# Moving two quantisation passes, eight PSUM conversions and one scaling between ScalarE and VectorE in a quantised matmul kernel with a recurrent branch

## The chip, the cores and the metric

The kernel runs on all 8 cores of one Trainium2 chip. Each core has its own TensorE (PE), VectorE (DVE), ScalarE (ACT), GpSimd (POOL) and SyncE (SP, which issues the transfers here). Every core gets 2 of the 16 sequences and runs the same program. The time is the device time in microseconds (us) of the slowest core.

## The reference, cut to what matters

```python
x = L0_attn_x                                   # (16, 2048, 2048) f32
xn = layernorm(x)
# branch 1: s
xn1 = layernorm(xn) * gamma + beta
u   = xn1 @ W_in + b_in                         # rank 8
h   = scan(u, sigmoid(decay_logit))             # h[t] = decay * h[t-1] + u[t]
x2  = xn + h @ W_out + b_out + xn1 * D_skip
xn2 = layernorm(x2) * gamma + beta
s   = x2 + relu(xn2 @ W_down + b_down) @ W_up + b_up     # rank 32
# branch 2: g
xq  = fake_quant(xn, 8 bits, per row)           # round(xn / scale) * scale
kq  = fake_quant(kernel, 8 bits, per column)    # 2048 x 2048
y   = relu(xq @ kq + fake_quant(bias))
g   = silu(fake_quant(y, 8 bits, per row))
out = x + s * g
```

## The kernel before, in words

A prologue of some 470 us loads and quantises the 2048x2048 weight matrix, which then stays in SBUF as `kq` (bf16), and folds the small weights together. After it a core handles its 4096 rows in 32 chunks of 128 rows, which lie on the 128 partitions. There is one stream of instructions for each engine, in the order in which the Python code emits them; each instruction waits on semaphores for the ones that it depends on. An engine never overtakes within its own stream, so an instruction that waits holds up all that was emitted for its engine behind it. The emission order, with the functions of the code, is:

```
emit_pro(0)
for c in range(NCH):
    emit_mid(c)
    emit_big_half(c, 0)
    emit_mid2(c)
    emit_big_evacs(c, 0)
    emit_big_half(c, 1)
    if c + 1 < NCH: emit_pro(c + 1)
    emit_big_evacs(c, 1)
    emit_echunk(c)
```

- `emit_pro(c)`: load of x; statistics on DVE (L450 to L465); square root on ACT (L466); the normalised row `xn` in f32 on ACT (L478), its bf16 copy `xnb` on ACT (L483); the row's largest magnitude on DVE (L484) and from it the two quantisation scales (L485 to L488; `inv0` is L487).
- `emit_mid(c)`: T1, 16 matmuls with the identity that transpose `xnb` (L518) into two PSUM banks in turn, four to a bank, each bank converted to bf16 in `xnT` by ACT (`t1e`, L522, four of them); `q8`, ACT's pass from `xn` to 8-bit integers (L525); `qbf`, ACT's pass from those to bf16 (L527); T2, 16 transposing matmuls of `qbf` (L539) through the same two banks, converted by ACT into `ixqT` (`t2e`, L543, four of them). A bank is written again only when its last conversion is done. Then a small transpose of the scale row, which ACT copies out (`auge`, L558), and behind that copy the small transpose `r1T` on PE (L560), copied by DVE (`r1a`, L561). Then PE multiplies `xnT` with the small weights (L578, 16 matmuls), DVE runs the scan (L590), and four rounds of two matmuls and two DVE operations (L609 to L617) make x2.
- `emit_big_half(c, h)`: 32 matmuls of 128x128 by 128x512 against one half of `kq` (L710) and two for the bias (L716). The first half waits for x2, the second one for the first one's evacuation.
- `emit_mid2(c)`: squares on ACT (L641), a square root, small matmuls, s = x2 + ... on DVE (L687).
- `emit_big_evacs(c, h)`: DVE scales the result of a half out of PSUM into `t1` with its row maximum (L727, L730).
- `emit_echunk(c)`: DVE makes the two scales (`g1` to `g6`, L774 to L779). Then, for each half of 1024 columns: `e2` rounds `t1` times a scale to int32 (`qi`, L783, DVE), `e3` is Relu to bf16 (L789, ACT), `e4` is Silu (L792, ACT), `sg` multiplies with s (L797, POOL), `o` adds x (L801, POOL), and a transfer stores it. There is one buffer `qi`, one `r` and one `g`: the second half's e2 waits for the first half's e3, its e4 for the first half's sg.

Because e4 of chunk c's second half is emitted for ACT ahead of all that `emit_mid(c+1)` emits for ACT, the conversions L522 of chunk c+1 stand behind it.

Of the kernel before, what the change touches and what calls it, by code (L numbers as in the profile page):

```python
# [11 lines left out]
OP = mybir.AluOpType  # L12
AF = mybir.ActivationFunctionType
# [67 lines left out]
def build_nc(n_seq, seq_len):  # L81
# [39 lines left out]
    with es:  # L121
# [32 lines left out]
        cq128 = sb("cq128", [128, 1], F32)  # L154
        cm128 = sb("cm128", [128, 1], F32)
# [16 lines left out]
        t1_t = sb("t1", [128, D], F32)  # L172
        qi_t = sb("qi", [128, 1024], I32)
# [176 lines left out]
        for fi in range(ND):  # L350
            h = {}
# [77 lines left out]
        def emit_pro(c):  # L429
# [58 lines left out]
            v4 = V([v1], lambda e: e.tensor_single_scalar(st[:, 12:13], st[:, 10:11], 1.0 / 127.0, OP.mult))  # L488
            rc["inv0"] = v3
            rc["sc0"] = v4  # L490
            return

        def emit_mid(c):
# [12 lines left out]
            for g in range(4):  # L506
                bank = tb2[g % 2]
                for b in range(4):
                    j = 4 * g + b
                    deps = [rc["xnbd"], L["eyeb"]]  # L510
                    if b == 0:
                        if g == 0:
                            deps.append(dep_pT0)
                        elif g == 1:
                            deps += dep_pT1
                        else:
                            deps.append(t1e[g - 2])
                    tlast = T(deps, lambda e, j=j, b=b, bank=bank: e.matmul(  # L518
                        bank[:, 128 * b:128 * (b + 1)], xnb_t[:, 128 * j:128 * (j + 1)], eyeb[:],
                        start=True, stop=True, skip_group_check=True), inc=(b == 3))  # L520
                t1e.append(S([tlast, dep_xnT_free],
                             lambda e, g=g, bank=bank: e.activation(xnT[:, 512 * g:512 * (g + 1)], bank[:], AF.Identity, bias=0.0, scale=1.0)))  # L522
            rc["t1b"] = tlast
            dep_u8 = R[c - 1].get("qbf") if c >= 1 else p_bq2
            rc["q8"] = S([rc["inv0"], dep_u8, c_q128], lambda e, xn=xn: e.activation(u8_t[:], xn[:], AF.Identity, bias=cq128[:], scale=st[:, 11:12]))  # L525
            dep_qbf = R[c - 1].get("t2b") if c >= 1 else KT0_FREE
            rc["qbf"] = S([rc["q8"], dep_qbf, c_m128], lambda e: e.activation(qbf_t[:], u8_t[:], AF.Identity, bias=cm128[:], scale=1.0))  # L527
            ixb = ixqT[c % 2]
            dep_ix_free = R[c - 2].get("bigb") if c >= 2 else (KT1_FREE if c == 0 else None)
            t2e = []  # L530
# [1 line left out]
            for g in range(4):  # L532
                bank = tb2[g % 2]
                for b in range(4):
                    j = 4 * g + b
                    deps = [rc["qbf"], L["eyeb"]]
                    if b == 0:
                        deps.append(t1e[g + 2] if g < 2 else t2e[g - 2])
                    tlast = T(deps, lambda e, j=j, b=b, bank=bank: e.matmul(  # L539
                        bank[:, 128 * b:128 * (b + 1)], qbf_t[:, 128 * j:128 * (j + 1)], eyeb[:],  # L540
                        start=True, stop=True, skip_group_check=True), inc=(b == 3))
                t2e.append(S([tlast, dep_ix_free],
                             lambda e, g=g, ixb=ixb, bank=bank: e.activation(ixb[:, 512 * g:512 * (g + 1)], bank[:], AF.Identity, bias=0.0, scale=1.0)))  # L543
            rc["t2b"] = tlast
            rc["t2e2"] = t2e[2]
            rc["t2e3"] = t2e[3]
# [190 lines left out]
        def emit_echunk(c):  # L737
            rc = R[c]
            st = st_t[c % 2]
            xb = x_t[c % 2]  # L740
            sb_ = s_t[c % 2]
            seq_, t0_ = c // CPS, (c % CPS) * CH
            if TRUNC >= 21:
                for h in range(2):
                    dep_o_free = R[c - 1].get(f"store{h}") if c >= 1 else None
                    oo = V(rc["last"] + [dep_o_free], lambda e, h=h: e.tensor_copy(
                        o_t[h][:], xn_t[c % 2][:, 1024 * h:1024 * (h + 1)]))
                    rc[f"store{h}"] = dma(f"d_o{h}", [oo], dout[seq_, t0_:t0_ + CH, 1024 * h:1024 * (h + 1)], o_t[h][:])
                rc["store"] = rc["store1"]
                return  # L750
            if TRUNC == 2:
                for h in range(2):
                    dep_o_free = R[c - 1].get(f"store{h}") if c >= 1 else None
                    oo = V([rc["s1"], dep_o_free], lambda e, h=h: e.tensor_copy(
                        o_t[h][:], sb_[:, 1024 * h:1024 * (h + 1)]))
                    rc[f"sg{h}"] = oo
                    rc[f"o{h}"] = oo
                    rc[f"store{h}"] = dma(f"d_o{h}", [oo], dout[seq_, t0_:t0_ + CH, 1024 * h:1024 * (h + 1)], o_t[h][:])
                rc["store"] = rc["store1"]
                return  # L760
            if TRUNC == 3:
                e1_ = rc["e1list"]
                for h in range(2):
                    dep_o_free = R[c - 1].get(f"store{h}") if c >= 1 else None
                    oo = V([e1_[2 * h + 1], dep_o_free], lambda e, h=h: e.tensor_copy(
                        o_t[h][:], t1_t[:, 1024 * h:1024 * (h + 1)]))
                    rc[f"o{h}"] = oo
                    if h == 1:
                        rc["e2b"] = oo
                    rc[f"store{h}"] = dma(f"d_o{h}", [oo], dout[seq_, t0_:t0_ + CH, 1024 * h:1024 * (h + 1)], o_t[h][:])  # L770
                rc["store"] = rc["store1"]
                return
            e1 = rc["e1list"]
            g1 = V([e1[3]], lambda e: e.reduce_max(st[:, 30:31], st[:, 26:30], axis=AX))  # L774
            g2 = V([g1], lambda e: e.tensor_single_scalar(st[:, 30:31], st[:, 30:31], 0.0, OP.max))
            g3 = V([g2], lambda e: e.tensor_single_scalar(st[:, 30:31], st[:, 30:31], 1e-30, OP.max))
            g4 = V([g3], lambda e: e.reciprocal(st[:, 31:32], st[:, 30:31]))
            g5 = V([g4], lambda e: e.tensor_single_scalar(st[:, 31:32], st[:, 31:32], 127.0, OP.mult))
            g6 = V([g3], lambda e: e.tensor_single_scalar(st[:, 30:31], st[:, 30:31], 1.0 / 127.0, OP.mult))  # L779
            seq, t0 = c // CPS, (c % CPS) * CH  # L780
            for h in range(2):
                dep_q_free = rc.get("e3_0") if h == 1 else (R[c - 1].get("e3_1") if c >= 1 else None)
                e2 = V([g5, e1[2 * h + 1], dep_q_free], lambda e, h=h: e.tensor_scalar(  # L783
                    qi_t[:], t1_t[:, 1024 * h:1024 * (h + 1)], st[:, 31:32], None, OP.mult))
                rc[f"e2_{h}"] = e2
                if h == 1:
                    rc["e2b"] = e2
                dep_r_free = rc.get("e4_0") if h == 1 else (R[c - 1].get("e4_1") if c >= 1 else None)
                e3 = S([e2, dep_r_free], lambda e: e.activation(r_t[:], qi_t[:], AF.Relu, bias=0.0, scale=1.0))  # L789
                rc[f"e3_{h}"] = e3  # L790
                dep_g_free = rc.get("sg0") if h == 1 else (R[c - 1].get("sg1") if c >= 1 else None)
                e4 = S([e3, g6, dep_g_free], lambda e: e.activation(  # L792
                    g_t[:], r_t[:], AF.Silu, bias=0.0, scale=st[:, 30:31]))
                rc[f"e4_{h}"] = e4
                if h == 1:
                    rc["e4b"] = e4
                sg = G([e4, rc["s1"], rc.get("tap_s")], lambda e, h=h: e.tensor_tensor(  # L797
                    sb_[:, 1024 * h:1024 * (h + 1)], g_t[:], sb_[:, 1024 * h:1024 * (h + 1)], OP.mult))
                rc[f"sg{h}"] = sg
                dep_o_free = R[c - 1].get(f"store{h}") if c >= 1 else None  # L800
                oo = G([sg, rc["xld"], dep_o_free], lambda e, h=h: e.tensor_tensor(  # L801
                    o_t[h][:], sb_[:, 1024 * h:1024 * (h + 1)],
                    xb[:, 1024 * h:1024 * (h + 1)], OP.add))
                rc[f"o{h}"] = oo
                rc[f"store{h}"] = dma(f"d_o{h}", [oo], dout[seq, t0:t0 + CH, 1024 * h:1024 * (h + 1)], o_t[h][:])
            rc["store"] = rc["store1"]
# [124 lines left out]
```

How the kernel before makes its waits and increments, by code:

```python
    def emit_engine(self, ename, eng, sems):  # L68
        for o in self.ops:
            if o["eng"] != ename:
                continue
            for k, v in o["waits"].items():
                eng.wait_ge(sems[k], v)
            inst = o["emit"](eng)
            if o["dma"] is not None:
                inst.then_inc(sems[o["dma"]], 16)
            elif o["inc"]:
                inst.then_inc(sems[ename], 1)
# [783 lines left out]
            @block.sync  # L862
            def _(sync):
                P.emit_engine("sync", sync, sems)
                sync.wait_ge(sems["d_o0"], 16 * NCH)
                sync.wait_ge(sems["d_o1"], 16 * NCH)
```

## Time and profile before

| | |
|---|---|
| median of 3 runs | 2776.59 us (2776.03 to 2780.07) |
| the profiled execution, its own time | 2776.11 us |
| span in its profile, slowest core (core 3) | 2774.6 us (cores 2771.2 to 2774.6) |
| busy of the span: PE, weight loads | 1423.6 us (51%), 592.1 us (21%) |
| busy of the span: DVE, ACT, POOL | 1029.1 us (37%), 807.5 us (29%), 298.6 us (11%) |
| TensorE clock granted, mean of the span | 0.692 of full speed |
| moved by the transfers | 84.75 MB, 9.3% of the 16 transfer engines' time |

A busy share is the part of the span in which an engine has an instruction in flight. No engine is busy much over half of the time here. A granted clock of 1.00 is 2.4 GHz and one of 0.50 is 1.2 GHz; a value between them is a mean over a stretch with both.

### The profile page before, as it was taken

The numbers are of one execution on the slowest core, as the hardware profiler recorded it, in microseconds if no ns is written. First come the engines' busy times: TensorE is split into PE (matmuls) and PEld (weight loads), VectorE is DVE, ScalarE is ACT, GpSimd is POOL, SyncE is SP. The second block draws the span as 40 slices with busy tenths as digits, with TensorE's granted clock in tenths as the row PEclk, the third lists the DMA queues.
The fourth block names the chain that finished last, engine by engine and source line by source line (L and its number), as shares of the span: only waits on it lengthen the run. The fifth ranks groups of instructions, "written<-read, shape, count | busy, mean of one in ns | idle before, by whom it ended". The sixth has DMA issues, their size and how long they took to land.

```text
span 2774.6 us, 30096 instructions; the slowest of 8 cores (2771.2 to 2774.6 us)
## 1 busy us (share of the span) xinstructions
PE 1423.6 (51%) x5025; PEld 592.1 (21%) x5025; DVE 1029.1 (37%) x2951; ACT 807.5 (29%) x964; POOL 298.6 (11%) x132
## 2 busy tenths in 40 slices
PE   1443333555555555555555555555555555555554
PEld 1222222222222222222222222222222222221221
DVE  4333333333333333333333333333333333333332
ACT  0111112233333332333333333333333333333331
POOL 0000000011111111111111111111111111111111
PEclk9999999866666666666666666666666666666666
DMA  1111111000000000000000000000000000000000
GB/s 37 37 46 40 39 44 46 2 30 31 31 31 31 31 31 31 31 31 31 31 31 31 31 31 31 31 31 31 31 31 31 31 31 31 31 31 31 31 16 16
DMA packets 56506, 86.68 MB, mean 31 GB/s; under 512 B 11118, under 2 KB 44014, under 8 KB 52206
## 3 DMA queue, kind: packets, MB, share of 16 engines
q1 hardware_dynamic: 56348, 84.75, 9.3%
q8 instruction: 77, 1.26, 0.2%
q14 instruction: 81, 0.66, 0.1%
HBM read 51.17 MB, written 33.55 MB: 31 GB/s over the span
## 4 chain that ended last, share of the span: by engine, by line
PE 32%; DVE 32%; ACT 15%; issue 15%; POOL 3%; DVEq 2%; SPq 1%; ACTq 0%; DMA 0%; POOLq 0%
PE py L710 12%; PE pb L578 4%; PE pb L539 4%; DVE x L617 3%; DVE x2tmp L616 3%; POOL s L797 3%; DVE t L450 3%; PE pb L410 3%; PE pb L376 3%; ACT xn L478 2%; ACT u L525 2%; DVE s L687 2%; ACT qbf L527 2%; PE pb L518 2%; DVE st L484 2%
## 5 line engine op out<-in xcount | busy, mean ns | idle before, releaser
L710 PE MATMUL py<-kq,ixqT 128*128 128x512 bf16 x2048 | 587.7, 458 | 153.7 <-DVE t L730 118.9
L797 POOL TENSOR_TENSOR s<-g,s 128x1024 f32<-128x1024 f32 x64 | 149.9, 2342 | 2455.0 <-ACT g L792 2455.0
L710 PEld LDWEIGHTS py<-kq,ixqT 128*128 128x128 bf16 x2048 | 229.9, 112 | 524.4 <-issue 362.2
L518 PE MATMUL pb<-eyeb,xnb 128*128 128x128 bf16 x512 | 116.9, 242 | 420.8 <-ACT xnT L522 351.5
L561 DVE CAST r1aug<-pff 1x128 bf16<-1x128 f32 x32 | 8.9, 279 | 601.3 <-PE pff L560 601.3
L641 ACT ACTIVATE sqscr<-x 128x512 f32<-128x512 f32 x128 | 80.6, 630 | 447.0 <-DVE x L617 445.7
L539 PE MATMUL pb<-eyeb,qbf 128*128 128x128 bf16 x512 | 122.8, 265 | 166.2 <-ACT qbf L527 164.3
L466 ACT ACTIVATE st<-nw 128x2 f32<-128x2 f32 x32 | 6.6, 205 | 653.9 <-DVE nw L465 653.9
L518 PEld LDWEIGHTS pb<-eyeb,xnb 128*128 128x128 bf16 x512 | 51.2, 100 | 496.0 <-issue 447.8
L801 POOL TENSOR_TENSOR o<-s,x 128x1024 f32<-128x1024 f32 x64 | 149.9, 2343 | 17.5 <-POOL s L797 17.5
L789 ACT ACTIVATE r<-qi 128x1024 bf16<-128x1024 int32 x64 | 67.6, 1056 | 198.8 <-DVE qi L783 195.8
L578 PE MATMUL pb<-xnT,wcat 128*96 128x128 bf16 x512 | 124.4, 312 | 0.7
L413 DVE CAST kq<-pb 128x512 bf16<-128x512 f32 x64 | 44.3, 692 | 161.0 <-PE pb L410 161.0
L539 PEld LDWEIGHTS pb<-eyeb,qbf 128*128 128x128 bf16 x512 | 53.4, 104 | 235.6 <-issue 185.3
L484 DVE TENSOR_REDUCE st<-xn 128x1 f32<-128x2048 f32 x32 | 73.2, 2286 | 77.3 <-ACT xn L478 77.3
L543 ACT ACTIVATE ixqT<-pb 128x512 bf16<-128x512 f32 x128 | 76.4, 597 | 78.8 <-PE pb L539 78.1
L609 PE MATMUL py<-outer_rhs,r1aug 2*128 2x512 bf16 x128 | 74.2, 580 | 44.7 <-DVE x2tmp L616 43.4
L617 DVE SCALAR_TENSOR_TENSOR x<-x2tmp,py 128x512 f32<-128x512 f32 x128 | 88.1, 688 | 22.5 <-DVE x2tmp L616 22.0
L616 DVE TENSOR_TENSOR x2tmp<-xn,py 128x512 f32<-128x512 f32 x128 | 88.0, 688 | 22.2 <-DVE x L617 20.5
L615 PE MATMUL py<-woutaug,haug 9*128 9x512 bf16 x128 | 75.7, 591 | 29.1 <-DVE x L617 29.1
L578 PEld LDWEIGHTS pb<-xnT,wcat 128*96 128x96 bf16 x512 | 78.9, 154 | 45.5 <-issue 2.9
L792 ACT ACTIVATE g<-r,st 128x1024 f32<-128x1024 bf16 x64 | 73.5, 1148 | 48.4 <-POOL s L797 48.0
(183 smaller groups left out, 1823.6 us busy)
## 6 DMA issues: line engine op xcount, KB each, us to landing
x<-L_attn_x SPq DMA_DIRECT2D x32, 1024.0 KB, 6.3
out<-o SPq DMA_DIRECT2D x64, 512.0 KB, 2.8
xn<-L_ffn_kernel SPq DMA_DIRECT2D x128, 64.0 KB, 2.0
s<-L_ffn_kernel SPq DMA_DIRECT2D x128, 64.0 KB, 2.0
wint<-L_attn_W_in SPq DMA_DIRECT2D x16, 4.0 KB
wdnt<-L_attn_W_down SPq DMA_DIRECT2D x16, 16.0 KB
x<-L_attn_W_up SPq DMA_DIRECT2D x1, 256.0 KB
eyef<-c_eye_f SPq DMA_DIRECT2D x1, 64.0 KB
```

Source lines behind the costliest of these rows:

```text
L376: tt = T(deps, lambda e, dj=dj, b=b, buf=buf: e.transpose(pb2[:, 128 * b:128 * (b + 1)], buf[:, 128 * dj:128 * (dj + 1)], eyef[:]), inc=(b ...
L410: tt = T(deps, lambda e, dj=dj, b=b, kqf=kqf: e.transpose(pbwd[:, 128 * b:128 * (b + 1)], kqf[:, 128 * dj:128 * (dj + 1)], eyef[:]), inc=( ...
L450: bn.append(V([rc["xld"], dep_st, dep_st2], lambda e, q=q: e.bn_stats(tb[:, 6 * q:6 * q + 6], xb[:, 512 * q:512 * (q + 1)])))
L484: rc["am"] = V([rc["xn"]], lambda e, xn=xn: e.reduce_max(st[:, 10:11], xn[:], axis=AX, apply_absolute_value=True))
L518: tlast = T(deps, lambda e, j=j, b=b, bank=bank: e.matmul(bank[:, 128 * b:128 * (b + 1)], xnb_t[:, 128 * j:128 * (j + 1)], eyeb[:], start= ...
L539: tlast = T(deps, lambda e, j=j, b=b, bank=bank: e.matmul(bank[:, 128 * b:128 * (b + 1)], qbf_t[:, 128 * j:128 * (j + 1)], eyeb[:], start= ...
L578: swu = T(deps, lambda e, j=j: e.matmul(pb3[0:96, 0:128], wcat[:, 96 * j:96 * (j + 1)], xnT[:, 128 * j:128 * (j + 1)], start=(j == 0), sto ...
L616: va = V([mo, rc["xn"], prev_b], lambda e, q=q, xn=xn: e.tensor_tensor(x2tmp[:], xn[:, 512 * q:512 * (q + 1)], py[0][:], OP.mult))
L617: vb = V([va, mx], lambda e, q=q: e.scalar_tensor_tensor(x2_t[:, 512 * q:512 * (q + 1)], x2tmp[:], 1.0, py[1][:], OP.mult, OP.add, accum_o ...
L710: mmlast = T(deps, lambda e, j=j, qq=qq, fofs=fofs, ixb=ixb: e.matmul(py[qq][:], ixb[:, 128 * j:128 * (j + 1)], kq[:, D * j + fofs:D * j + ...
L797: sg = G([e4, rc["s1"], rc.get("tap_s")], lambda e, h=h: e.tensor_tensor(sb_[:, 1024 * h:1024 * (h + 1)], g_t[:], sb_[:, 1024 * h:1024 * ( ...
L801: oo = G([sg, rc["xld"], dep_o_free], lambda e, h=h: e.tensor_tensor(o_t[h][:], sb_[:, 1024 * h:1024 * (h + 1)], xb[:, 1024 * h:1024 * (h ...
```

## The change

Three things change.

- `q8` and `qbf` are emitted at the end of `emit_pro` instead of in the middle of `emit_mid`: for ACT they now stand ahead of `emit_echunk` of the chunk before, and not behind it. They stay on ACT and keep their operands and waits.
- The eight conversions out of PSUM for each chunk, `t1e` and `t2e`, go from ACT (`activation`, Identity) to DVE (`tensor_copy`).
- `e2`, the scaling from f32 to int32 of 1024 columns, two for each chunk, goes from DVE (`tensor_scalar`) to ACT (`activation`, Identity, with the scale as a column of values).

```diff
 # emit_pro(c)
             rc["inv0"] = v3
             rc["sc0"] = v4
+            dep_u8 = R[c - 1].get("qbf") if c >= 1 else p_bq2
+            rc["q8"] = S([v3, dep_u8, c_q128], lambda e, xn=xn: e.activation(u8_t[:], xn[:], AF.Identity, bias=cq128[:], scale=st[:, 11:12]))
+            dep_qbf = R[c - 1].get("t2b") if c >= 1 else KT0_FREE
+            rc["qbf"] = S([rc["q8"], dep_qbf, c_m128], lambda e: e.activation(qbf_t[:], u8_t[:], AF.Identity, bias=cm128[:], scale=1.0))
             return
 # emit_mid(c)
-                t1e.append(S([tlast, dep_xnT_free],
-                             lambda e, g=g, bank=bank: e.activation(xnT[:, 512 * g:512 * (g + 1)], bank[:], AF.Identity, bias=0.0, scale=1.0)))
+                t1e.append(V([tlast, dep_xnT_free],
+                             lambda e, g=g, bank=bank: e.tensor_copy(xnT[:, 512 * g:512 * (g + 1)], bank[:])))
             rc["t1b"] = tlast
-            dep_u8 = R[c - 1].get("qbf") if c >= 1 else p_bq2
-            rc["q8"] = S([rc["inv0"], dep_u8, c_q128], lambda e, xn=xn: e.activation(u8_t[:], xn[:], AF.Identity, bias=cq128[:], scale=st[:, 11:12]))
-            dep_qbf = R[c - 1].get("t2b") if c >= 1 else KT0_FREE
-            rc["qbf"] = S([rc["q8"], dep_qbf, c_m128], lambda e: e.activation(qbf_t[:], u8_t[:], AF.Identity, bias=cm128[:], scale=1.0))
 ...
-                t2e.append(S([tlast, dep_ix_free],
-                             lambda e, g=g, ixb=ixb, bank=bank: e.activation(ixb[:, 512 * g:512 * (g + 1)], bank[:], AF.Identity, bias=0.0, scale=1.0)))
+                t2e.append(V([tlast, dep_ix_free],
+                             lambda e, g=g, ixb=ixb, bank=bank: e.tensor_copy(ixb[:, 512 * g:512 * (g + 1)], bank[:])))
 # emit_echunk(c)
-                e2 = V([g5, e1[2 * h + 1], dep_q_free], lambda e, h=h: e.tensor_scalar(
-                    qi_t[:], t1_t[:, 1024 * h:1024 * (h + 1)], st[:, 31:32], None, OP.mult))
+                e2 = S([g5, e1[2 * h + 1], dep_q_free], lambda e, h=h: e.activation(
+                    qi_t[:], t1_t[:, 1024 * h:1024 * (h + 1)], AF.Identity, bias=0.0, scale=st[:, 31:32]))
```

## Rows read from the trace of the kernel before

**Rows 1.** The page: part 4, the chain by engine; part 5, the matmuls L710

```profile
PE 32%; DVE 32%; ACT 15%; issue 15%; POOL 3%; DVEq 2%; SPq 1%; ACTq 0%; DMA 0%; POOLq 0%
...
L710 PE MATMUL py<-kq,ixqT 128*128 128x512 bf16 x2048 | 587.7, 458 | 153.7 <-DVE t L730 118.9
```

**Rows 2.** One line, L560: ns min/median/max, first and last start (us), forms

```profile
L560 PE MATMUL pff<-eyef,st x32: 369/369/373, 493.6 to 2708.9; 128*1 128x128 f32 x32
```

**Rows 3.** Timeline of ACT in one chunk: start us, us, instruction [idle before <-releaser]

```profile
1535.29 2.10 ACT L478 ACTIVATE xn<-x,st 128x2048 f32<-128x2048 f32 x1 [0.73 <-DVE st L469]
1544.74 1.06 ACT L789 ACTIVATE r<-qi 128x1024 bf16<-128x1024 int32 x1 [5.30 <-DVE qi L783]
1545.99 1.28 ACT L792 ACT_TABLE_LOAD   x1 [0.19 <-ACT r L789]
1547.28 1.15 ACT L792 ACTIVATE g<-r,st 128x1024 f32<-128x1024 bf16 x1
...
1551.07 1.15 ACT L792 ACTIVATE g<-r,st 128x1024 f32<-128x1024 bf16 x1 [1.49 <-POOL s L797]
1552.12 1.07 ACT L522 ACTIVATE xnT<-pb 128x512 bf16<-128x512 f32 x2
...
1555.63 2.08 ACT L525 ACTIVATE u<-xn,cq,st 128x2048 uint8<-128x2048 f32 x1
1557.92 2.00 ACT L527 ACTIVATE qbf<-u,cm 128x2048 bf16<-128x2048 uint8 x1 [0.20 <-ACT u L525]
...
1564.71 0.25 ACT L558 ACTIVATE augrow<-pff 1x128 bf16<-1x128 f32 x1
```

**Rows 4.** Timeline of DVE in the same chunk

```profile
1540.41 0.15 DVE L487 TENSOR_SCALAR st<-st 128x1 f32<-128x1 f32 x1
...
1543.62 0.15 DVE L779 TENSOR_SCALAR st<-st 128x1 f32<-128x1 f32 x1
1543.85 0.75 DVE L783 TENSOR_SCALAR qi<-t,st 128x1024 int32<-128x1024 f32 x1
...
1565.75 0.28 DVE L561 CAST r1aug<-pff 1x128 bf16<-1x128 f32 x1 [19.09 <-PE pff L560]
```

**Rows 5.** Timeline of PE in the same chunk

```profile
1539.69 1.97 PE L518 MATMUL pb<-eyeb,xnb 128*128 128x128 bf16 x8 [1.48 <-ACT xnb L483]
1553.11 1.94 PE L518 MATMUL pb<-eyeb,xnb 128*128 128x128 bf16 x8 [11.44 <-ACT xnT L522]
1560.17 3.94 PE L539 MATMUL pb<-eyeb,qbf 128*128 128x128 bf16 x16 [5.13 <-ACT qbf L527]
...
1565.21 0.37 PE L560 MATMUL pff<-eyef,st 128*1 128x128 f32 x1 [0.76 <-ACT augrow L558]
```

**Rows 6.** Timeline of POOL in the same chunk

```profile
1548.63 2.34 POOL L797 TENSOR_TENSOR s<-g,s 128x1024 f32<-128x1024 f32 x1 [61.31 <-ACT g L792]
```

**Rows 7.** One line, L413 of the prologue: ns min/median/max, first and last start, forms

```profile
L413 DVE CAST kq<-pb x64: 690/692/693, 94.9 to 466.7; 128x512 bf16<-128x512 f32 x64
```

**Rows 8.** Windows: us, busy (instructions) PE PEld DVE ACT POOL, granted clock, DMA, GB/s

```profile
1541.70:1553.00 11.30, 0.00 (x0) 0.00 (x0) 3.05 (x10) 6.47 (x7) 4.10 (x2) 0.53 0.00 0
...
1570.50:1580.90 10.40, 4.78 (x10) 0.89 (x10) 7.63 (x20) 2.17 (x6) 0.00 (x0) 0.50 0.00 1
1580.90:1591.40 10.50, 10.47 (x35) 3.90 (x35) 1.35 (x9) 2.21 (x4) 0.00 (x0) 0.72 0.01 2
```

**Rows 9.** Timeline of PE: three of the 64 big halves, the longest and one short pair

```profile
1010.77 10.01 PE L710 MATMUL py<-kq,ixqT 128*128 128x512 bf16 x32 [1.08 <-DVE x L617]
...
1439.01 9.23 PE L710 MATMUL py<-kq,ixqT 128*128 128x512 bf16 x32 [1.07 <-DVE x L617]
1457.76 8.40 PE L710 MATMUL py<-kq,ixqT 128*128 128x512 bf16 x32 [4.29 <-DVE t L730]
```

**Rows 10.** Timeline of chunk 0: DVE's L487 and ACT's L525

```profile
480.12 0.15 DVE L487 TENSOR_SCALAR st<-st 128x1 f32<-128x1 f32 x1
...
484.03 2.08 ACT L525 ACTIVATE u<-xn,cq,st 128x2048 uint8<-128x2048 f32 x1
```

## The prediction, written before the changed kernel ran

> **What bounds the kernel now.** I read four views, in this order. First the page: the chain that ended last is split over PE, DVE and ACT, with 15% of "issue" [rows 1], so no engine is the bound. What bounds is a chain through all of them, 32 times over. Second, one line that runs once in each chunk gives the period: the scale transpose L560 goes from 493.6 to 2708.9 us in 31 steps [rows 2], so (2708.9 - 493.6) / 31 = 71.46 us for a chunk. Third, the timelines of a chunk in mid-span, engine by engine [rows 3 to 6], of which I follow the stretch from `xn` of chunk c+1 (L478, 1535.29) to its `r1T` (L560, 1565.21), 29.92 us. All edits fall into it; from `r1T` round to the next `xn` the code stays as it is. Fourth, the windows: for 11.3 us of that stretch PE has no instruction at all, and the clock falls to 0.5 [rows 8].
>
> Within it the reader sees one long detour on ACT. `inv0`, all that `q8` needs beside `xn`, is ready at 1540.41 + 0.15 = 1540.56 [rows 4]. But `q8` (L525) starts at 1555.63 [rows 3], 15 us later, since it stands on ACT behind chunk c's epilogue: e3, a table load, e4, and the second e4, which waits 1.49 us for POOL's sg [rows 3, 6]. T1's second half waits 11.44 us for a conversion out of the same queue, and T2 waits 5.13 us for `qbf` [rows 5]. In that time DVE does nothing but the two e2; before L561 it had been idle 19.09 us [rows 4].
>
> **Hand-overs, from the same rows.** DVE to ACT 0.14 (L783 ends 1544.60, L789 starts 1544.74); ACT to a dependent ACT 0.21 (L525 to L527); ACT to POOL 0.20 (first e4 ends 1548.43, sg starts 1548.63); POOL to ACT 0.10 (1550.97 to 1551.07); ACT to PE 0.25 (L558 ends 1564.96, L560 starts 1565.21) [rows 3 to 6].
>
> **The change, part by part.** Before, the stretch runs: e2 at 1543.85, e3, load, e4, sg, second e4 to 1552.22, T1's last two banks with their conversions, `q8` and `qbf` (4.3 us), T2 (3.94), `auge`, `r1T` at 1565.21.
>
> *ACT after the change.* Its queue is xn, xnb, q8, qbf, e2, e3, load, e4, e2, e3, e4, auge. From inv0, and with the hand-overs above:
> - q8 1540.76 to 1542.84, qbf 1543.05 to 1545.05 (2.08, 2.00 [rows 3]). xnb is out of the way: PE starts on it at 1539.69 [rows 5].
> - first e2 from 1545.05. No row shows f32 to int32 on ACT. Bounds: below 0.75, what it takes on DVE [rows 4]; above 2.08, what twice the elements take from f32 to integers [rows 3]. Nearest are 1.06 (L789, 1024 elements, constants) and 1.15 (L792, 1024 elements, its scale a column) [rows 3]. I take 1.15, as e2's scale is a column: to 1546.20. It waits for g5, which is done before L779 at 1543.62 [rows 4], so that wait is covered by qbf.
> - e3 1546.40 to 1547.46 (1.06), load 1547.65 to 1548.93 (1.28), e4 to 1550.09 (1.15), POOL's sg 1550.29 to 1552.63 (2.34 [rows 6]).
> - meanwhile the second e2 (to 1551.24) and e3 (1551.44 to 1552.50). The second e4 waits for both sg and e3, which release it within 0.1 us of each other: 1552.73 to 1553.88.
> - auge to 1554.13 (0.25), r1T on PE at 1554.38.
>
> Putting q8 and qbf ahead of e2 thus makes the epilogue late by 1.7 us (second e4 1552.73 for 1551.07). The output and the load of x behind it are late by as much. POOL had been idle 61.31 us before its sg [rows 6], and no instruction of the stretch waits for x, so that costs nothing.
>
> *PE and DVE after the change.* `t1e` stands on DVE behind g6, which ends at 1543.77 [rows 4]. A conversion of a 128x512 PSUM bank to bf16 on DVE took 0.69 in the prologue [rows 7]; bounds are 0.28 (L561, one partition [rows 4]) and 0.75 (L783). I take 0.69: it is the same operation and shape. So t1e 1543.85 to 1544.54, T1's third bank 1544.8 to 1545.8 (4 x 0.245, from 1.94 for 8 [rows 5]), its conversion to 1546.6, T2's first bank 1546.85 to 1547.85 (qbf has been there since 1545.05), its conversion to 1548.7, T2's third bank to 1549.9, its last to 1550.9, the scale transpose to 1551.3. This branch is 2.6 us ahead of auge (1553.88). Eight conversions on DVE are therefore hidden by ACT's epilogue; without that cover r1T would start 2.4 us earlier still. What is queued behind a waiting conversion on DVE is L561 and the recurrent branch, which need T2 to be over anyway.
>
> *Sum.* A chunk gets shorter by 1565.21 - 1554.38 = 10.83 us, up to 11.0 where independent ACT instructions overlap a little, as L522 and the e4 ahead of it do by 0.1 [rows 3]. I take 10.9. It holds for 31 chunks: 337.9 us. Chunk 0 has no epilogue ahead of it: there q8 moves only from 484.03 to 480.12 + 0.15 + 0.2 = 480.47 [rows 10], 3.5 us. The last epilogue gets longer by the slower e2, 1.15 + 0.2 for 0.75 + 0.14: 0.5 us. The span goes from 2774.6 to 2774.6 - 337.9 - 3.5 + 0.5 = 2433.7 us. The profiled execution took 2776.11 in all, 1.5 more than its span and 0.5 below the median of the runs, so the forecast is **2435 us**.
>
> *The clock.* The matmuls L710 take 587.7 / 32 = 18.37 us of a chunk [rows 1]; each half starts at 0.5 and rises to 1.0 on its way (the mean of a first half's window is 0.72 [rows 8]). Nothing between r1T and the halves changes, and there the clock is at 0.5 now [rows 8], so I leave it. But halves vary with where the rise falls: a pair took as little as 17.63, and the longest half 10.01 [rows 9]. With another period that mix can shift: at most 32 x (18.37 - 17.63) = 24 us down, and 32 x (20.02 - 18.37) = 53 us up. T1 does not care: 8 of its matmuls took 1.97 us right behind a big half and 1.94 after the long idle [rows 5].
>
> **The rivals.**
> - *The clock is up sooner.* With PE's idle stretch of 11.3 us gone, over which the mean clock is 0.53 [rows 8], the 2.4 GHz level might last or return before the first half. The first half's window of 10.5 us at 0.72 is 7.6 us of work at full clock, so 2.9 us less for each chunk: 2435 - 32 x 2.9 = 2342. Against it: in the 10.4 us ahead of the half the clock is 0.50 with PE 46% busy [rows 8], and that stretch is untouched. The Trainium skill ("TensorE: Matmul & The Clock Gate", section "Loop structure matters more than you think") has it that the loop nest decides whether matmuls stay warm, and that long waits between bursts let the clock drop; by that rule this case would be the likelier one, and the idle stretch of the trace agrees with it.
> - *DVE and POOL disturb each other.* No row here shows both at work, because POOL's sg runs while DVE idles. After the change T2's conversions lie over the first sg. The least is nothing; if sg took twice its 2.34, auge would be late by 2.34: 2435 + 31 x 2.34 = 2508.
> - *e2 brings table loads.* If ACT had to load a table for the second e2, between two Silus, and another one to return, both would lie ahead of the second e4. The time from the first e4's end to the second's start would be 1.47 (load) + 1.35 (e2) + 1.06 (e3) + 1.47 (load) = 5.35 instead of 2.64: 31 x 2.7 = 84 us, so 2519. Against it: L522, Identity too, follows e4 with no load between [rows 3]. The Trainium skill ("ScalarE: Activation LUTs", section "What ACT_TABLE_LOAD costs") puts a switch of tables at about 2.66 us with a drain; the rows show 1.28 plus 0.19 and e4 right behind [rows 3]. By the page's price this rival would be 31 x (2 x 2.66 + 2.41 - 2.64) = 158 us, an estimate, so 2593.
> - *The low clock throughout.* If the halves never rose, 7.6 us of work a half would take 15.2, about 30.4 less 18.37 and less the bias matmuls, roughly 11 us for each chunk: gone is the whole gain, 2780, no change. Nothing in the rows speaks for it: the rise comes within the half itself.
> - *Slower: the conversions on DVE are the new chain.* The eight go one after another from 1543.85, and L561 stands behind them, at 1565.75 now. It is late from (1565.75 - 1543.85) / 8 = 2.74 us for each conversion on. At 3 us L561 starts at 1567.85, and the time is 2776 + 31 x 2.1 = 2841. Against it: 0.69 at 64 out of 64 [rows 7]; up to about 1.38 they would even be free, since L561 is then not due before 1554.9.
>
> **How the numbers follow.** Forecast 80%; clock up sooner 4%; DVE against POOL 8%; table loads 3%; low clock throughout 2%; conversions as the chain 2%; and 1% that gain and loss cancel in some other way. The forecast's own range is 2435 - 24 - 12 (e2 at its lower bound, 0.4 for each chunk) = 2399 to 2435 + 53 = 2488 at the outmost; both clock ends need all 32 chunks at their extreme, so I take 2403 to 2480. It holds about 0.75 of the forecast's 0.80 and the milder half of the DVE/POOL case. Under 0.2% (5.6 us) a measurement of this kernel can't be told from no change. Faster by more: all but the last three cases, 0.95. Within 0.2%: 0.02. Slower: 0.03.
>
> **What would show it.** In the changed trace: the L560 period near 60.6 us; L525 right behind `inv0`, at xn + 5.5 us; e2 as an ACT row of 1.15 with no table load of its own, the loads staying at two for each chunk; the first e3 at about xn + 11.1; L560 idle before and released by ACT's auge, not by a conversion; conversions of 0.69 on DVE; sg still 2.34. The prediction is wrong if sg or the conversions stretch when they overlap, if the big halves' share moves from 18.4 us a chunk, or if another wait (x late, the store) turns up ahead of L450 or L478.

## The result, and the profile after

The changed kernel takes 2361.34 us (median of 10 runs, 2356.9 to 2401.21; seven of them lie between 2356.9 and 2366) against 2776.55 us, a ratio of 0.8501 with a 95% interval of 0.8483 to 0.852. The forecast was 2435 in 2403 to 2480: the direction was right, the gain 74 us larger than forecast, and the time lies outside the range.

In the two slowest executions (2397.24 and 2401.21 us) and, by 0.9%, in the profiled one, the cores of one die took longer at a lower granted clock, so all that follows is read on core 5, of the other die, in every kernel. The median of the eight executions under 2390 us is 2357.6, the 2357 of the expectations below. In the kernel before, cores 3 and 5 agree: the periods are 71.46 and 71.38 us.

The period first, by L560 on core 5 (ns min/median/max, first and last start), the changed kernel:

```profile
L560 PE MATMUL pff<-eyef,st x32: 369/372/373, 489.8 to 2287.7; 128*1 128x128 f32 x32
```

(2287.7 - 489.8) / 31 = 58.00 us for a chunk. For [rows 2] the same core of the kernel before has 492.8 to 2705.7, 71.38 us. The gain is 13.39 us a chunk where 10.9 were forecast.

The timeline of ACT in one chunk of the changed kernel, which answers [rows 3]:

```profile
1572.29 2.10 ACT L478 ACTIVATE xn<-x,st 128x2048 f32<-128x2048 f32 x1 [0.73 <-DVE st L469]
...
1577.71 2.10 ACT L492 ACTIVATE u<-xn,cq,st 128x2048 uint8<-128x2048 f32 x1 [1.27 <-DVE st L488]
...
1581.92 1.14 ACT L783 ACTIVATE qi<-t,st 128x1024 int32<-128x1024 f32 x1
1583.15 1.06 ACT L789 ACTIVATE r<-qi 128x1024 bf16<-128x1024 int32 x1
1584.39 1.28 ACT L792 ACT_TABLE_LOAD   x1 [0.19 <-ACT r L789]
...
1589.48 1.15 ACT L792 ACTIVATE g<-r,st 128x1024 f32<-128x1024 bf16 x1 [0.45 <-POOL s L797]
1590.53 0.25 ACT L558 ACTIVATE augrow<-pff 1x128 bf16<-1x128 f32 x1
```

This stretch is as forecast, nearly to the tenth: q8 at xn + 5.42 (5.47 forecast), the first e3 at xn + 10.86 (11.11), e2 1.14 us with no table load of its own (1.15), the second e4 at xn + 17.19 (17.44).

PE and DVE on the other side of `r1T`, same chunk, PE first, against [rows 4, 5]:

```profile
1576.80 2.05 PE L522 MATMUL pb<-eyeb,xnb 128*128 128x128 bf16 x8 [0.64 <-DVE st L484]
1581.63 2.02 PE L522 MATMUL pb<-eyeb,xnb 128*128 128x128 bf16 x8 [2.78 <-DVE xnT L526]
1583.72 4.15 PE L539 MATMUL pb<-eyeb,qbf 128*128 128x128 bf16 x16
...
1591.04 0.37 PE L560 MATMUL pff<-eyef,st 128*1 128x128 f32 x1 [2.67 <-ACT augrow L558]
...
1592.19 2.26 PE L578 MATMUL pb<-xnT,wcat 128*96 128x128 bf16 x16
```

```profile
1587.98 0.69 DVE L543 CAST ixqT<-pb 128x512 bf16<-128x512 f32 x1 [0.34 <-PE pb L539]
1591.58 0.28 DVE L561 CAST r1aug<-pff 1x128 bf16<-1x128 f32 x1 [2.91 <-PE pff L560]
...
1595.66 1.31 DVE L586 TENSOR_SCALAR u_sb<-u_sb,c 8x128 f32<-8x128 f32 x1
```

PE sits idle for 2.67 us ahead of L560 and is released by ACT's auge, not by a conversion, and the conversions take 0.69: both as forecast. Two rows are new. The 16 matmuls L578 take 2.26 us; in the kernel before it was 3.83 to 3.86, here in one chunk of core 5:

```profile
1563.23 3.86 PE L578 MATMUL pb<-xnT,wcat 128*96 128x128 bf16 x16
```

And L586, which touches 8 partitions by 128 elements, takes 1.31 us.

**Where the gain lies.** The table gives each stage as the difference of the starts of its two lines in core 5's timelines, mean of 31 chunks, in us. L584 is DVE's copy of L578's result, L616 its first operation of the four rounds that make x2, and L654 a small transpose that PE runs right behind the first big half.

| stage | before | after | difference | forecast |
|---|---|---|---|---|
| `inv0` (L487) to `r1T` (L560) | 24.70 | 13.67 | -11.03 | -10.9 |
| L578 to L584 | 4.28 | 2.63 | -1.65 | 0 |
| L584 to the scan L590 | 1.23 | 2.19 | +0.96 | 0 |
| L590 to L616 | 2.11 | 2.08 | -0.03 | 0 |
| L616 to the first big half | 7.03 | 6.75 | -0.28 | 0 |
| first big half to L654 | 10.12 | 9.11 | -1.01 | 0 |
| L654 to L687 | 4.50 | 4.21 | -0.29 | 0 |
| L687 round to `inv0`, and L560 to L578 | 17.41 | 17.34 | -0.07 | 0 |

So the forecast stretch holds, and 2.4 us a chunk come from stages whose code wasn't touched, net of one that became slower. Three causes are to be found: L578, L586, and the first big half.

**A first reading that fell.** The obvious one is the rival "the clock is up sooner". The window over L578's 16 matmuls (us, busy and instructions for PE, PEld, DVE, ACT, POOL, granted clock, DMA) speaks against it, in the changed kernel on core 5:

```profile
1592.19:1594.45 2.26, 2.26 (x18) 2.08 (x17) 0.00 (x0) 0.00 (x0) 2.10 (x1) 0.50 0.57 232
```

They go at 1.2 GHz, as before, 0.126 us apart, where they had been 0.232 apart. What differs stands in no row that the forecast read. Before, each L578 waits on two semaphores: that of ACT, for its conversion, and that of DVE, for its weights. With the conversions on DVE both are one semaphore, and the program's bookkeeping keeps only the larger value: one wait. In the trace's records of the kernel before the two waits ahead of an L578 lie 0.106 us apart, on PE's own queue.

### The profile page after: what moved, and what is told of

It reads as the page before. It is cut to its first block, busy times and chain, and to the rows that moved or that the text cites. A ratio compares the mean times of both kernels' runs of the same rounds, so it can differ in the third digit from the quotient of the medians.

```text
span 2375.1 us, 27628 instructions; the slowest of 8 cores (2352.5 to 2375.1 us)
## 1 busy us (share of the span) xinstructions
PE 1385.5 (58%) x5025; PEld 582.0 (25%) x5025; DVE 1185.0 (50%) x3143; ACT 732.3 (31%) x772; POOL 298.8 (13%) x132
## 4 chain that ended last, share of the span: by engine, by line
DVE 36%; PE 29%; issue 16%; ACT 12%; POOL 3%; DVEq 2%; SPq 1%; ACTq 0%; DMA 0%; POOLq 0%
PE py L710 14%; DVE x2tmp L616 4%; DVE x L617 4%; POOL s L797 3%; PE pb L410 3%; PE pb L376 3%; PE pb L578 3%; DVE s L687 3%; DVE t L450 3%; DVE st L484 3%; ACT xn L478 3%; DVEq L73 2%; DVE t L727 2%; DVE u_sb L586 2%; ACT g L792 2%
## 5 line engine op out<-in xcount | busy, mean ns | idle before, releaser
L710 PE MATMUL py<-kq,ixqT 128*128 128x512 bf16 x2048 | 611.3, 472 | 159.4 <-DVE t L730 128.2
L797 POOL TENSOR_TENSOR s<-g,s 128x1024 f32<-128x1024 f32 x64 | 150.2, 2346 | 2055.0 <-ACT g L792 2005.7
L710 PEld LDWEIGHTS py<-kq,ixqT 128*128 128x128 bf16 x2048 | 237.6, 116 | 538.7 <-issue 438.2
L801 POOL TENSOR_TENSOR o<-s,x 128x1024 f32<-128x1024 f32 x64 | 149.7, 2340 | 17.5 <-POOL s L797 17.5
L413 DVE CAST kq<-pb 128x512 bf16<-128x512 f32 x64 | 44.3, 692 | 161.0 <-PE pb L410 161.0
L543 DVE CAST ixqT<-pb 128x512 bf16<-128x512 f32 x128 | 88.6, 692 | 49.5 <-PE pb L539 49.5
L655 DVE CAST r2row<-pff 1x128 bf16<-1x128 f32 x32 | 8.9, 279 | 195.8 <-PE pff L654 195.8
L526 DVE CAST xnT<-pb 128x512 bf16<-128x512 f32 x128 | 85.6, 689 | 33.1 <-PE pb L522 32.5
L615 PE MATMUL py<-woutaug,haug 9*128 9x512 bf16 x128 | 75.8, 592 | 39.8 <-DVE x L617 39.8
L616 DVE TENSOR_TENSOR x2tmp<-xn,py 128x512 f32<-128x512 f32 x128 | 88.0, 688 | 11.5 <-PE py L615 0.6
L410 PE MATMUL pb<-eyef,xn 128*128 128x128 f32 x128 | 37.4, 442 | 94.7 <-ACT xn L396 72.1
L410 PE MATMUL pb<-eyef,s 128*128 128x128 f32 x128 | 37.4, 441 | 94.3 <-ACT s L396 71.7
L609 PE MATMUL py<-outer_rhs,r1aug 2*128 2x512 bf16 x128 | 74.9, 585 | 29.1 <-DVE x2tmp L616 22.3
L783 ACT ACTIVATE qi<-t,st 128x1024 int32<-128x1024 f32 x64 | 72.5, 1133 | 28.0 <-DVE st L779 28.0
L492 ACT ACTIVATE u<-xn,cq,st 128x2048 uint8<-128x2048 f32 x32 | 67.0, 2093 | 41.6 <-DVE st L488 41.6
```

Of the source, the lines that this page charges most:

```text
L410: tt = T(deps, lambda e, dj=dj, b=b, kqf=kqf: e.transpose(pbwd[:, 128 * b:128 * (b + 1)], kqf[:, 128 * dj:128 * (dj + 1)], eyef[:]), inc=( ...
L526: lambda e, g=g, bank=bank: e.tensor_copy(xnT[:, 512 * g:512 * (g + 1)], bank[:])))
L543: lambda e, g=g, ixb=ixb, bank=bank: e.tensor_copy(ixb[:, 512 * g:512 * (g + 1)], bank[:])))
L616: va = V([mo, rc["xn"], prev_b], lambda e, q=q, xn=xn: e.tensor_tensor(x2tmp[:], xn[:, 512 * q:512 * (q + 1)], py[0][:], OP.mult))
L710: mmlast = T(deps, lambda e, j=j, qq=qq, fofs=fofs, ixb=ixb: e.matmul(py[qq][:], ixb[:, 128 * j:128 * (j + 1)], kq[:, D * j + fofs:D * j + ...
```

## The experiments

Each theory had a name in the expectations: "waits" (a wait costs PE's queue about 0.1 us, even one that is long satisfied), "port" (DVE is held by POOL), "place of the rise" (where in a big half the clock goes up). "First half" is the stretch from the first big half's start to L654. A ratio is to the kernel before, run beside it.

**1. One wait less, in the kernel before.**

```diff
-                deps = [t1e[j // 4], p_wcat[3 * j], p_wcat[3 * j + 1], p_wcat[3 * j + 2]]
+                deps = [t1e[j // 4], p_wcat[-1] if j == 0 else None]
```

> The kernel before, with one edit: the 16 matmuls L578 wait for the conversion of their columns and no longer each for the weights too (the first one waits once for the last of the weight preparation). So they wait on one semaphore each instead of two, as in the changed kernel. Theory 'waits': each wait that TensorE's queue carries costs it about 0.106 us, so the stretch from the first L578 to L584 shrinks from 4.28 to about 2.65 us at an unchanged granted clock, and the time falls by 32 x 1.6 = 51 us to 2725, give or take what the big halves do. Rival 'clock': the stretch got shorter because TensorE's clock was up; then nothing changes here, 2776.

Measured: 2695.79 us, ratio 0.9712 (0.9687 to 0.9737). L578 to L584 went from 4.28 to 2.68 us, with the conversions still on ACT. The row of the 16 matmuls on core 5:

```profile
1527.78 2.26 PE L578 MATMUL pb<-xnT,wcat 128*96 128x128 bf16 x16
```

"Waits" holds: (4.28 - 2.68) / 16 = 0.10 us for each wait. The gain is 80 us where that explains 50. The rest is the first big half, which fell from 10.12 to 9.32 us to L654 though nothing near it was touched.

**2. The wait put back, in the changed kernel.**

```diff
-                deps = [t1e[j // 4], p_wcat[3 * j], p_wcat[3 * j + 1], p_wcat[3 * j + 2]]
+                deps = [t1e[j // 4], rc["qbf"], p_wcat[3 * j + 1], p_wcat[3 * j + 2]]
```

> The changed kernel, with one wait added to each of the 16 matmuls L578: on a ScalarE instruction (qbf) that has long been over, so that each waits on two semaphores again as in the kernel before. Nothing else differs. Theory 'waits': L578 to L584 goes from 2.63 back to 4.28 us; VectorE's L586 then starts when GpSimd is through and no longer waits 0.96 us for it. Net 31 x (1.65 - 0.96) = 21 us slower, 2357 to 2379. Rival 'clock': a satisfied wait costs nothing, 2357.

Measured: 2394.33 us, ratio 0.8624 (0.8609 to 0.8638), so 33 to 37 us slower than the changed kernel. L578 to L584 is back at 4.29, and L584 to L590 at 1.22, as expected. The 15 us beyond the forecast are again the first big half: 9.59 for 9.11. That L586 is fast again when it comes 1.65 us later is the first support for "port".

**3 to 5. Each edit alone, on the kernel before** (the diff is the change's own, in parts).

> The kernel before with the first edit alone: q8 and qbf emitted at the end of emit_pro; conversions stay on ScalarE, e2 on VectorE. By the forecast's own accounting: the epilogue is late by 0.3, the conversions L522 and L543 still stand behind the second e4 and are now the chain, r1T comes at xn + 25.1 instead of xn + 29.9: 31 x 4.8 = 149 us, 2628. Rival: the move is the whole of the change's gain, about 2440. In both, from L578 to L584 it takes 4.28 us as before, since conversions and weights are on two semaphores.

> The kernel before with the second edit alone: the eight conversions on VectorE. q8 starts when the second e4 is over (xn + 16.8), r1T comes at xn + 26.5 instead of 29.9: 3.4 us for each chunk. Theory 'waits': besides, the matmuls that wait for a conversion and for the weights now wait on one semaphore, which takes 1.65 us off L578 and about 0.6 off the rounds behind it: 31 x (3.4 + 2.2) = 174 us, 2602. Without that theory: 31 x 3.4 = 105, 2671.

> The kernel before with the third edit alone: e2 on ScalarE. It takes 1.15 for 0.75 us and the first one is on the chain: 0.4 to 0.5 us for each chunk, 2776 + 31 x 0.45 = 2790. Rival: ScalarE needs table loads around it, 31 x 2.7 more, 2870. Rival: hidden, 2776.

| | measured, ratio (interval) | `inv0` to `r1T` | L578 to L584 | first half to L654 |
|---|---|---|---|---|
| q8 and qbf moved | 2589.17, 0.9319 (0.9303 to 0.9335) | 19.74 | 4.28 | 9.30 |
| conversions on DVE | 2574.73, 0.9267 (0.9248 to 0.9285) | 21.64 | 2.62 | 9.17 |
| e2 on ACT | 2783.61, 1.0025 (1.0015 to 1.0035) | 25.04 | 4.29 | 10.11 |

The move alone takes 4.96 us off the chain (4.8 expected), the conversions alone 3.06 (3.4), e2 alone adds 0.34 (0.4 to 0.5). In sum 7.7, and together 11.03: as long as either q8 or the conversions stand behind the epilogue on ACT, ACT holds the chunk, and only with both away is the rest of the queue all that r1T waits for. The shorter L578 comes with the conversions alone, as "waits" has it. And the first half is near 9.2 in both kernels that became faster, 10.11 in the one that didn't; no expectation had that, which is most of why the first two came in 39 and 27 us under the 2628 and 2602 expected.

**6. The changed kernel with e2 back on DVE.**

> The changed kernel without its third edit: e2 back on VectorE. There the second e2 waits for e3 and holds up the conversions behind it, which start 3.2 us later (xn + 11.8 for xn + 8.6); their branch, 2.6 us ahead before, is now the later one by 0.7: 31 x 0.7 = 22 us slower than the changed kernel, 2379. Rival: e2 is better off on VectorE, as it is faster there (0.75 for 1.13) and the epilogue starts 1.3 us sooner: 2357 - 40 = 2317.

Measured: 2356.92 us, ratio 0.8489 (0.8475 to 0.8503), no change. `inv0` to `r1T` is 0.86 longer (14.53), as expected; but L584 to L590 is 0.93 shorter (1.26). r1T comes later, and L586 with it, after POOL's last instruction. The third edit is thus worth nothing here: what it gains on the chain it loses waiting for POOL. The 2379 expected had the longer branch right and left that wait out.

**7. auge on DVE, in the changed kernel.**

```diff
-            rc["auge"] = S([rc["augT"], dep_aug_free],
-                           lambda e: e.activation(augrow[c % 2][:], prow[:], AF.Identity, bias=0.0, scale=1.0))
+            rc["auge"] = V([rc["augT"], dep_aug_free],
+                           lambda e: e.tensor_copy(augrow[c % 2][:], prow[:]))
```

> The changed kernel with the copy auge (L558) on VectorE instead of ScalarE, so that r1T no longer stands behind the epilogue. Theory: ScalarE's epilogue is what holds r1T, which now comes 2.4 us sooner. Theory 'port': VectorE's instructions with one SBUF input wait for GpSimd's running instruction to end. Then L586 and the cast L593 behind it, both ahead of GpSimd's end now, wait for it, and of the 2.4 us only 0.8 are left: 31 x 0.8 = 25 us, 2332. Rival, no such wait (L586 was slow for another reason): 31 x 2.4 = 74 us, 2283.

Measured: 2355.05 us, ratio 0.8497 (0.8471 to 0.8522), no change against the changed kernel. `inv0` to `r1T` fell from 13.67 to 11.80, so ACT's epilogue was what held it. Of these 1.87 us, 1.15 were lost one stage on, where DVE waits for POOL: L590 to L616 grew from 2.08 to 3.90, and L584 to L590 fell from 2.19 to 1.52. The expectation had the same 0.8 or so left by then. Another 0.61 went to the first half, 9.72 for 9.11, and that it had not. DVE and then POOL, one chunk of this run:

```profile
1535.17 0.72 DVE L586 TENSOR_SCALAR u_sb<-u_sb,c 8x128 f32<-8x128 f32 x1
1535.99 0.47 DVE L590 TENSOR_TENSOR_SCAN h<-decay_rep,h,u_sb 8x128 f32<-8x128 f32 x1
1536.63 2.04 DVE L593 CAST haug<-h 8x128 bf16<-8x128 f32 x1 [0.17 <-DVE h L590]
```

```profile
1533.47 2.34 POOL L797 TENSOR_TENSOR s<-g,s 128x1024 f32<-128x1024 f32 x1
1536.08 2.52 POOL L801 TENSOR_TENSOR o<-s,x 128x1024 f32<-128x1024 f32 x1 [0.27 <-POOL s L797]
```

L586 ends at 1535.89, 0.08 after POOL's L797 (1535.81). L593, issued while L801 runs, ends at 1538.67, 0.07 after it (1538.60), and takes 2.04 us where it took 0.21. Only L590, which got in between the two, ran at once, and in this chunk L801, which started while it ran, took 2.52 for 2.34.

**8. L586 in another form, in the changed kernel.**

```diff
-            uc = V([um, p_c8], lambda e: e.tensor_scalar(u_sb[0:8, :], u_sb[0:8, :], c8[:], None, OP.add))
+            uc = V([um, p_c8, p_z8], lambda e: e.scalar_tensor_tensor(u_sb[0:8, :], u_sb[0:8, :], c8[:], zero8[:], OP.add, OP.add))
```

> The changed kernel with L586 in another form: scalar_tensor_tensor with a second SBUF input of zeros, instead of tensor_scalar with one input; same values. Theory 'port': only the form with one SBUF input waits for GpSimd. Then L586 takes 0.3 instead of 1.2 us on average and the chunk is 0.9 us shorter: 2357 - 29 = 2328. Rival: any VectorE instruction out of SBUF waits for GpSimd; then the new form waits as long, 2357.

Measured: 2357.07 us, ratio 0.8491 (0.8478 to 0.8503), no change. Its row (the new line is L588):

```profile
1540.01 1.41 DVE L588 SCALAR_TENSOR_TENSOR u_sb<-u_sb,c,zero 8x128 f32<-8x128 f32 x1
```

The form with two SBUF inputs waits as well; in the one chunk in which POOL is idle it takes 0.34. "Port" fell in the version stated here, that only the form with one SBUF input waits. But L585, one input from SBUF and one from PSUM, took 0.28 while POOL was at work, and the conversions out of PSUM that ran beside POOL kept their 0.69. I stated it anew: what waits has nothing but SBUF on its input side.

**9. Those inputs moved to PSUM, and the cast to ACT, in the changed kernel.**

```diff
+        pu = pff[0][0:8, 256:384]
-            um = V([...], lambda e: e.tensor_tensor(u_sb[0:8, :], u_sb[0:8, :], prep1[0:8, :], OP.mult))
-            uc = V([um, p_c8], lambda e: e.tensor_scalar(u_sb[0:8, :], u_sb[0:8, :], c8[:], None, OP.add))
+            um = V([...], lambda e: e.tensor_tensor(pu[:], u_sb[0:8, :], prep1[0:8, :], OP.mult))
+            uc = V([um, p_c8], lambda e: e.tensor_scalar(pu[:], pu[:], c8[:], None, OP.add))
...
-            rc["hb"] = V([...], lambda e, hb_=hb_: e.tensor_copy(haug[0:8, :], hb_[:]))
+            rc["hb"] = S([...], lambda e, hb_=hb_: e.activation(haug[0:8, :], hb_[:], AF.Identity, bias=0.0, scale=1.0))
```

The scan reads `pu` too.

> The changed kernel with the recurrent branch's small VectorE operations kept off pairs of SBUF reads: the product (L585) and the sum (L586) go to a free corner of a PSUM bank, the scan reads its input from there, and the cast to haug (L593) goes to ScalarE. Same values. Theory 'port': only VectorE instructions that read SBUF through two ports (two SBUF inputs, or one in the fast form) wait for GpSimd; those with PSUM on one side don't. Then L584 to L590 goes from 2.19 to 1.2 us, the ScalarE cast costs 0.2, net 31 x 0.75 = 23 us: 2334. Rival: whatever reads SBUF waits for GpSimd; then the scan waits in L586's place, 2357 or a little more.

Measured: 2354.33 us, ratio 0.8472 (0.8458 to 0.8486). POOL and DVE in one chunk (lines are one further on):

```profile
1536.59 2.34 POOL L802 TENSOR_TENSOR o<-s,x 128x1024 f32<-128x1024 f32 x1 [0.27 <-POOL s L798]
...
1537.63 0.35 DVE L587 TENSOR_SCALAR pff<-pff,c 8x128 f32<-8x128 f32 x1
1538.08 0.47 DVE L591 TENSOR_TENSOR_SCAN h<-decay_rep,h,pff 8x128 f32<-8x128 f32 x1
```

Both run inside POOL's instruction now: L584 to L590 fell from 2.19 to 1.32 us, which shows the wait. The time didn't follow to the 2334 expected, since the first half grew from 9.11 to 9.79: 0.87 won, 0.17 paid for the cast on ACT, 0.68 lost to the clock, which rose later in it.

**10. The same, and auge on DVE.**

> The same, and auge (L558) on VectorE as in the earlier experiment that gained nothing. Theory: that one gained nothing because the 1.9 us by which r1T came sooner were spent waiting for GpSimd in L586 and L593; with those waits gone they count: 2334 - 31 x 1.9 = 2275. Rival: another wait on GpSimd's or ScalarE's epilogue takes their place, about 2334.

Measured: 2307.55 us, ratio 0.8287 (0.8235 to 0.8338). Now the 1.8 us of experiment 7 count (`inv0` to `r1T` 11.84, L590 to L616 2.25). The period fell from 57.99 to 56.05 us, and that is the 1.8 and 0.13 in the first half. The four executions scatter (2293.98 to 2337.77), so the median says less than usual: the profiled one took 2294.54. That is still above the 2275 expected, which started from 2334; the first half stayed at 9.66.

**11. Longer on purpose, the kernel before.**

```diff
+            dly = S([rc["augT"], ...], lambda e, xn=xn: e.activation(sqscr[:], xn[:, 0:512], AF.Identity, bias=0.0, scale=1.0))
+            dly = S([dly], lambda e, xn=xn: e.activation(sqscr[:], xn[:, 0:512], AF.Identity, bias=0.0, scale=1.0))
-            rc["auge"] = S([rc["augT"], dep_aug_free],
+            rc["auge"] = S([dly, rc["augT"], dep_aug_free],
```

> The kernel before, made longer on purpose: two extra ScalarE passes over 512 columns into a scratch tile stand ahead of auge (L558) on the chain, about 1.5 us for each chunk. Nothing else differs. Theory 'place of the rise': with a period of 71.4 to 71.7 us the TensorE clock rises late in nearly every first half (first L710 to L654 takes 10.1 us), and with any other period seen so far it rises earlier (9.2 to 9.3). Then that stretch falls to about 9.3 here too, and of the 1.5 us only 0.7 are paid: 2776 + 31 x 0.7 = 2798. Rival: the stretch is shorter in the changed kernel because TensorE is busier ahead of it; then it stays at 10.1 here and the time is 2776 + 31 x 1.5 = 2822.

Measured: 2790.01 us, ratio 1.0057 (1.0036 to 1.0077). `inv0` to `r1T` became 1.52 us longer, the first half to L654 0.94 shorter (9.18). Windows from the half's start in steps of 3 us, PE alone (us, busy, granted clock), and ahead of them the 15.39 us before it. First the kernel before:

```profile
1562.36:1577.75 15.39, 9.15 (x28) 0.50 0.00 1
...
1577.75:1580.75 3.00, 3.00 (x8) 0.50 0.02 5
1580.75:1583.75 3.00, 3.00 (x9) 0.52 0.00 0
```

Then the one with the delay:

```profile
1570.00:1585.39 15.39, 9.15 (x28) 0.50 0.00 1
...
1585.39:1588.39 3.00, 3.00 (x8) 0.50 0.03 5
1588.39:1591.39 3.00, 3.00 (x14) 0.92 0.00 0
```

PE did exactly the same in the 15.39 us ahead, at the same level. In the one kernel the clock rises some 5.9 us into the half, in the other 3.2. So the shorter half isn't earned by a busier PE in that stretch; what differs is when the half starts. My statement of it was too simple, though: the delayed kernel's period, 71.81, is next to that of experiment 5 (71.70), whose half took 10.11. It isn't the period alone. And the second big half went the other way: 8.67 us before, 9.69 here (means of 32 chunks, core 5).

**12. All of 10, and no wait on PE that an earlier one covers.**

```diff
             for k, v in o["waits"].items():
+                if ename == "tensor" and seen.get(k, 0) >= v:
+                    continue
+                seen[k] = max(seen.get(k, 0), v)
                 eng.wait_ge(sems[k], v)
```

> The same, and TensorE's queue carries no wait that an earlier wait of its own on the same semaphore already covers. Theory 'waits': a wait costs TensorE's queue about 0.106 us even where it is long satisfied. The transposes (two waits for each of 32) and L578 (one for each of 16) come closer together: L578 to L584 from 2.60 to about 2.1, T1 and T2 together about 1.0 sooner as their banks' conversions allow: 31 x 1.5 = 46 us off the run before it, about 2230. The big halves stay as they are: their matmuls of 512 columns are 0.216 us apart at full clock with or without waits.

Measured: 2184.34 us, ratio 0.7859 (0.7839 to 0.7879): 7.5% under the changed kernel, and 110 us under experiment 10 if the two profiled executions are compared (2294.54 and 2184.10). The transposes are the clearest rows, the first eight of T1 at full clock and eight of T2 (lines are five further on):

```profile
1520.46 0.61 PE L527 MATMUL pb<-eyeb,xnb 128*128 128x128 bf16 x8 [1.58 <-ACT xnb L488]
...
1527.04 1.18 PE L544 MATMUL pb<-eyeb,qbf 128*128 128x128 bf16 x8 [0.35 <-DVE xnT L531]
```

0.61 us for eight where it was 1.97 [rows 5]. `inv0` to `r1T` fell from 11.84 to 9.70, L578 to L584 from 2.62 to 2.32. I had expected 1.5 us a chunk and got 2.6, since the transposes' stage gained twice as much (2.1 for 1.0); and the prologue, which has such waits too, gave another 28: the first L560 comes at 461.6 us instead of 490.0.

## Why the prediction was wrong

- *The bound and the chain*: right. The stretch from `xn` to `r1T` was the place, and its new length was met within 0.13 us: `inv0` to `r1T` -11.03, forecast -10.9.
- *q8 and qbf ahead of e2, the epilogue late*: right; the second e4 came at xn + 17.19, the forecast said 17.44.
- *Conversions on DVE at 0.69, hidden by ACT's epilogue; r1T released by auge*: right (0.69, idle 2.67 us by auge). "Without that cover r1T would start 2.4 us earlier" was tried in experiment 7: it is 1.9.
- *e2 at 1.15 on ACT without table loads*: right, 1.14.
- *The step that failed* is the one that left all else alone: "from `r1T` round to the next `xn` the code stays as it is", and with it "Nothing between r1T and the halves changes". The code stayed, its waits didn't. A result that changes its engine changes its semaphore, and the 16 matmuls L578 of a chunk lost a wait each in PE's queue, at 0.10 us: 1.65 us (experiments 1 and 2), which is 31 x 1.65 = 51 of the 74 us. The 0.28 before the big half goes with the same edit (it is there with the conversions alone, 6.75, and not with the move alone, 7.03). The trace has four waits fewer there for each chunk, at L609 and L615; that it is the waits too was not tried separately. The matmuls L710 lost 63 waits a chunk and gained nothing by it: at full clock they are 0.216 us apart in both kernels.
- *The sentence on T1*, "T1 does not care" for the clock, had the right rows and the wrong lesson. Eight matmuls took 1.97 us at full clock and 1.94 at half since PE's queue held them, at two waits each; free of them they took 0.61 (experiment 12).
- *The first big half*: -1.01 us a chunk, 31 us. This is the second step that failed, and it is a path that was wrong. The forecast took both halves together (18.37 us of a chunk), made their mix the source of the range, and put its mean at no change. Together they did not change: 18.33 us before and 18.46 after, for the 32 matmuls L710 of either half on core 5, means of 32 chunks. But the late rise of the clock moved from the first half (9.66 to 8.64) to the second (8.67 to 9.82), here in one chunk of each kernel, before and after:

```profile
1577.75 9.95 PE L710 MATMUL py<-kq,ixqT 128*128 128x512 bf16 x32 [1.08 <-DVE x L617]
...
1597.43 8.66 PE L710 MATMUL py<-kq,ixqT 128*128 128x512 bf16 x32 [3.66 <-DVE t L730]
```

```profile
1605.84 8.62 PE L710 MATMUL py<-kq,ixqT 128*128 128x512 bf16 x32 [0.98 <-DVE x L617]
...
1623.88 9.82 PE L710 MATMUL py<-kq,ixqT 128*128 128x512 bf16 x32 [4.09 <-DVE t L730]
```

Only the first half is on the chain: in experiment 1 the matmuls of the second took 9.53, 0.86 us more than before, and neither the stretch from L687 to `inv0` nor that from `inv0` to `r1T` grew by more than 0.05. Part of the gain is therefore luck of the start: the first half is 9.17 to 9.32 in experiments 1, 3, 4 and 11, and 9.66 to 9.79 in 7, 9, 10 and 12.

- *DVE and POOL*: the rival had the right pair and the wrong victim. POOL's sg kept its 2.34 us; DVE waited. It cost 0.96 us, 30 us in all, and hid behind the two gains. In the changed kernel L586 thus waits for POOL's last instruction, however much sooner it could start. That is why experiments 6 and 8 changed nothing, and it is most of what experiment 7 lost; the rest of that went to the first half.
- *The rival "the clock is up sooner"* came near the time (2342) by luck: it wanted the high level to last or return before the first half, worth 2.9 us, and from L560 to the first half the granted clock is 0.50 in both kernels, in every chunk but the first. What came sooner is the rise within the half, 1.01 us, and experiment 11 has that too with the idle stretch left open. The Trainium skill ("TensorE: Matmul & The Clock Gate", section "Loop structure matters more than you think") has it that a long wait between matmuls lets the clock drop. The kernel before agrees with it, 0.53 over its idle stretch [rows 8]; but with PE's longest wait in T1 down from 11.44 to 2.78 us the clock still stood at 0.50 when the first half began.
- In sum, in us a chunk: 10.9 forecast, +0.13 on it, +1.65, +0.28, +0.29 and +0.10 (waits and clock in small stages), +1.01, -0.96: 13.4. Times 31, with 3 us for chunk 0 and the tail: 418, which takes 2776 to 2358.

Open stays what sets the place of the clock's rise (experiment 11 excludes PE's work in the 15.39 us ahead of the half and the period alone), and why DVE waits for POOL: the runs show for which instructions, not on what.

## What to carry to other kernels

When an instruction changes its engine, list who waits for it and on which semaphores they wait then: waits that merge or split are paid in the consumer's queue, and short matmuls feel them, while those of 512 columns hide them. A matmul stage whose spacing is the same at both clock levels, as T1's was, is worth a look at its waits. Before filling an idle engine, look at what runs beside it: a tiny VectorE instruction on SBUF alone can last as long as GpSimd's next 128x1024 pass does. And for a gain or loss of about 1 us a chunk, check where the clock rises in the big bursts, and which of them is on the chain, before crediting an edit with it.

## What the runs showed of the hardware

- A satisfied semaphore wait costs TensorE's queue 0.10 us: L578's matmuls are 0.232 us apart with two waits, 0.126 with one (1.2 GHz), while 512-column matmuls are 0.216 apart (2.4 GHz) with one or two; eight 128x128 transposes take 1.97 us with two waits each and 0.61 with almost none, both at a granted clock of 1.00.
- The VectorE instructions here with all inputs in SBUF ended 0.07 to 0.14 us after the GpSimd instruction that was running when they came (L586 1.31 for 0.28, L593 2.04 for 0.21, the form with two inputs 1.41 for 0.34); those with an input in PSUM didn't wait (0.28, 0.35, 0.47).
- With the same work on TensorE in the 15.39 us ahead, the clock rose 5.9 us into a burst in one kernel and 3.2 us in another that starts it at another moment, worth 0.94 us; the next burst went the other way, 8.67 and 9.69 us.
